# Two steps moved inside the period of an attention and FFN kernel: the denominators' reciprocals behind the first norm, the queries' transposes behind the last down tile

## The reference

```python
def layer(h, p):
    q = _phi((h @ wq + bq_).reshape(b, s, H, DH))       # _phi(t) = elu(t) + 1, 16 heads of 8
    k = _phi((h @ wk + bk_).reshape(b, s, H, DH))
    v = (h @ wv + bv_).reshape(b, s, H, DH)
    kv = jnp.einsum('bshd,bshm->bhdm', k, v)
    z = 1.0 / (jnp.einsum('bshd,bhd->bsh', q, k.sum(axis=1)) + 1e-06)
    att = jnp.einsum('bshd,bhdm,bsh->bshm', q, kv, z).reshape(b, s, d)
    h = h + att @ wo + bo_
    h = _ln(h, g1_, be1_)                               # the first norm
    y = jax.nn.gelu(h @ w1 + c1_, approximate=False) @ w2 + c2_
    return (_ln(h + y, g2_, be2_), None)                # the second norm
...
    xn = _layernorm(x, axis=-1)
    s = ...  # eight layers on xn, and a last _ln
    g = _silu(...)  # routed experts on xn
    return x + s * g
```

## Time and profile before

| what | us |
|---|---|
| median of 3 runs | 873.08 |
| lowest and highest run | 872.48 and 874.48 |
| the profiled execution | 874.67 |
| its span in the trace | 873.0 |
| TensorE, VectorE, ScalarE busy | 818.8, 795.7, 720.0 |
| mean granted clock of TensorE | 0.972 of full speed |

### The profile page before, as it was taken

One profiled execution on the slowest core, in us unless ns is written; L12 is line 12 of the kernel. 1 busy time (PEld: TensorE's weight loads), 2 busy tenths in 40 slices (PEclk: granted clock), 3 DMA queues, 4 the chain that ended last, 5 costly groups with the idle time before them and its releaser, 6 DMA issues.

```text
span 873.0 us, 19269 instructions
## 1 busy us (share of the span) xinstructions
PE 818.8 (94%) x5914; PEld 742.1 (85%) x5914; DVE 795.7 (91%) x2763; ACT 720.0 (82%) x1271; POOL 376.9 (43%) x362
## 2 busy tenths in 40 slices
PE   5698999999999999999999999999999999977776
PEld 4588899999999999999998999999999999876653
DVE  6888999989899999989899999989999989999998
ACT  2579999989998899989998899889998999654543
POOL 5234445445454444445445445354443544332113
PEclk9899999999999999999999999999999999999995
DMA  5300201010010101020010101010010000000002
GB/s 146 88 2 2 43 2 24 12 29 16 2 34 2 43 2 35 1 44 2 2 34 2 44 1 35 1 44 2 1 35 1 1 2 1 20 7 1 1 1 97
DMA packets 26264, 18.76 MB, mean 21 GB/s; under 512 B 4354, under 2 KB 22195, under 8 KB 26164
## 3 DMA queue, kind: packets, MB, share of 16 engines
q1 hardware_dynamic: 25300, 16.95, 7.4%
q10 hardware_dynamic: 864, 0.59, 0.2%
HBM read 15.43 MB, written 2.10 MB: 20 GB/s over the span
## 4 chain that ended last, share of the span: by engine, by line
PE 77%; DVE 14%; ACT 5%; issue 4%; DMA 0%; ACTq 0%; DVEq 0%
PE down_ps L749 20%; PE small_ps L682 6%; PE att_ps L712 6%; PE up_ps L741 5%; PE up_ps L739 5%; PE up_ps L740 5%; PE t_ps L660 4%; PE t_ps L719 3%; PE kq_ps L672 3%; PE kq_ps L673 3%; PE kq_ps L674 3%; DVE z_lo L1001 2%; ACT z_hi L900 2%; PE up_ps L703 2%; PE small_ps L690 2%
## 5 line engine op out<-in xcount | busy, mean ns | idle before, releaser
L749 PE MATMUL down_ps<-w_use,hid 128*128 128x128 f32 x2048 | 261.3, 276 | 0.7 <-ACT hid L851 0.7
L749 PEld LDWEIGHTS down_ps<-w_use,hid 128*128 128x128 f32 x2048 | 245.8, 193 | 1.9 <-ACT hid L851 1.1
L1019 POOL TENSOR_TENSOR res_ffn<-z_tm,g_ffn 128x512 f32<-128x512 f32 x64 | 82.7, 1292 | 265.4 <-DVE k_e L1103 240.9
L1008 POOL TENSOR_TENSOR res_att<-z_tm,g_att 128x512 f32<-128x512 f32 x64 | 82.5, 1288 | 174.3 <-DVE h L961 174.3
L851 ACT ACTIVATE hid<-up_ps 128x512 f32<-128x512 f32 x192 | 113.7, 592 | 30.7 <-PE up_ps L741 23.2
L973 DVE BATCH_NORM_STATS2 st<-h 128x6 f32<-128x128 f32 x512 | 109.1, 275 | 0.1
L906 ACT ACTIVATE z_tm<-h,shift,rstd 128x128 f32<-128x128 f32 x224 | 91.7, 482 | 0.0
L739 PE MATMUL up_ps<-z_hi,w_hi 128*128 128x512 f32 x192 | 86.2, 449 | 0.7 <-DVE z_lo L1001 0.7
L1022 POOL TENSOR_TENSOR res_ffn<-res_ffn,ffn_row 128x512 f32<-128x512 f32 x64 | 84.2, 1315 | 5.0
L1011 POOL TENSOR_TENSOR res_att<-res_att,att_row 128x512 f32<-128x512 f32 x64 | 82.4, 1287 | 5.0
L672 PE MATMUL kq_ps<-w_kq_hi,zq_hi 128*128 128x256 f32 x256 | 83.0, 324 | 1.5 <-DVE zq_lo L921 1.5
(11 more groups left out here) (191 smaller groups left out, 1964.8 us busy)
## 6 DMA issues: line engine op xcount, KB each, us to landing
raw_w<-in_L_attn_W SPq DMA_DIRECT2D x15, 256.0 KB, 4.6
out_y<-gate_tm SPq DMA_DIRECT2D x8, 256.0 KB, 2.2
bias_bc<-in_L_attn_c SPq DMA_DIRECT2D x7, 256.0 KB, 4.5
x_tm<-in_L_attn_x SPq DMA_DIRECT2D x3, 512.0 KB, 7.8
raw_rows<-in_L_attn_be SPq DMA_DIRECT2D x15, 64.0 KB, 4.1
raw_g<-in_L_attn_g SPq DMA_DIRECT2D x14, 64.0 KB, 3.2
x_tm<-in_L_attn_x SPq DMA_DIRECT2D x2, 256.0 KB, 3.3
raw_rows<-in_L_attn_bo SPq DMA_DIRECT2D x8, 64.0 KB, 4.1
```

The costliest lines, as they stand in the source:

```text
L749: last = nc.tensor.matmul(down_ps[:, t, :], hid[:, j, t * P:(t + 1) * P], w2_use[:, j, :], start=(j == 0), stop=(j == FC - 1))
```

## The change

Two calls are moved, and no instruction is added, removed or altered. On VectorE `dve_rden` goes from behind `dve_blocks` to behind `dve_norm1`. On TensorE `pe_qn_transpose` goes from before the fourth down tile to behind it. Their waits go with them. The queues of ScalarE, GpSimd and SyncE are as before.

```diff
@@ pe_period
                 pe_z1_transpose(pe, p - 1, p + 2 if state else UNITS)
+            if ffn:
+                pe_down(pe, p - 2, (3,))
             if att:
                 pe_qn_transpose(pe, p)
-            if ffn:
-                pe_down(pe, p - 2, (3,))
             if state:
@@ dve_period
                 dve_den(dve, p)
                 dve_blocks(dve, p)
-                dve_rden(dve, p)
             if b == 4 and is_layer(l + 1):
@@ dve_period
             if ln1:
                 dve_norm1(dve, p, p - 1)
             if att:
+                dve_rden(dve, p)
                 dve_q_n(dve, p)
                 dve_kvo(dve, p)
```

## The result

| | before | after |
|---|---|---|
| median of the runs, us | 873.78 (4 runs) | 894.50 (4 runs) |
| lowest and highest, us | 872.48, 875.23 | 893.31, 894.74 |
| profiled execution, us | 874.67 | 894.54 |
| its span, us | 873.0 | 892.8 |

The ratio of the runs is 1.0234, with a 95% interval from 1.0214 to 1.0254. The changed kernel is slower, inside the range of the prediction, 5 us above its value.

The account below looks back on a forecast made before the run. It took TensorE's hand-overs through ScalarE and VectorE as the bound, with ScalarE nearly as long. Six layers at +2.66, +0.8, +1.0 and -1.4 gave +16.4 on 874.67: 891.1 profiled, 889.5 us median; range 881 to 896.

Parts of the forecast that it names:

- The ring L719, z_hi, z_lo, L660: TensorE to ScalarE to VectorE and back: 2.01 us of hand-overs, plus 9.80 of TensorE, make the 11.81 us period.
- q_n starts at Z + 1.95: ScalarE's copy of the transposed queries starts 1.95 us after Z, the start of L719; 0.82 later than before.
- ScalarE has 0.59 of room: ScalarE's slack per plain period: 0.45 us idle before z_hi plus 0.14 at the second GELU, against q_n's 0.82 delay.
- its ring through rstd is 12.00: From q_n through rstd's Exp, m_r, norm and L719 back to q_n: no period after the change under 12.00 us.
- The sign of being wrong that I had named: On ScalarE, z_hi still idle by about 0.45 us in plain periods would mean room the forecast had not seen.
- the period with the rounding of W1: Period where ScalarE also rounds W1 ahead of its table load: some 0.53 us more, 12.53 us.
- The attention product waits 0.11 to 0.12 for q_n: On TensorE, L712 starts at Z + 2.61 against 2.50, adding 0.11 to 0.12 us wherever nothing else is late.
- The reciprocals behind the norm make z_lo late in a period that starts right with the norm: On VectorE, 0.69 us of reciprocals put z_lo at Z + 1.68 instead of 1.26, L660 at 2.43 instead of 2.01.
- A layer: plus 2.66: Eight periods of a middle layer walked to 99.22 us after against 96.56 before; bounds 2.3 to 3.1.
- Outside the middle layers: First layer: nothing up to about 94 us, then +0.8; last layer: first three periods +1.0, last five -1.4 us.
- TensorE's waits are taken away: Rival: TensorE is the bound and loses its waits at L703 and for the norm; at most -8.6 us, 864.5; 3%.
- The clock falls: Rival: TensorE waits in most periods, so 3% of the span runs at 1.2 GHz; +13 us, about 903; 4%.

Follow-up runs that it names:

- the short copy: Changed kernel (both moves) with ScalarE's copy q_n (L893) cut to a quarter of its columns: 886.90 us, ratio 1.0156.
- the short norm: Changed kernel (both moves) with two of the four tiles of ScalarE's second norm (L906) left out: 892.37 us, ratio 1.0208.

## Why the prediction held, and where its steps did not

The sign, the size and the range held: 891.1 was summed for the profiled execution, 894.54 measured. The account of the light periods did not hold, and that the sum came so near is in part luck. Step by step:

- *The ring L719, z_hi, z_lo, L660 bounds the kernel before, and TensorE's 9.80 us outside it.* Shown for the plain period: 0.22 us taken out of the 9.80 shorten it from 11.81 to 11.59. Two periods of a layer are held by the norm instead.
- *q_n starts at Z + 1.95.* Right: L703 at 1.33, q_n at 1.97 (432.14 against 430.17), idle before it for L703 59 times, 45.2 us in all.
- *ScalarE has 0.59 of room, and its ring through rstd is 12.00.* Wrong, and this was the step that carried my account of the light periods. I read the 0.68 between two GELUs as ScalarE's own time. It was TensorE's pace; ScalarE needs 0.48. From q_n to the Exp of rstd it takes 7.83 in the plain period that begins at 418.05 (420.01 to 427.84), and not 8.22. With 7.83 that ring is 11.61 us, less than the 11.81 of the period before the change, and ScalarE's room is 0.45 + 0.53 = 0.98 instead of 0.59, more than the 0.82 by which q_n is later. The sign of being wrong that I had named is there: z_hi still sits idle 0.47 in the plain period (430.81). m_r waits for rstd 30 times in 64, 12.3 us in all, and not every time, and the period with the rounding of W1, for which I had 12.53, takes 12.12. Relieving ScalarE of 0.77 us gave 0.38 a layer.
- *The attention product waits 0.11 to 0.12 for q_n.* The mechanism was right and its size was off. It was listed as a small bound, and it is the cost of the light periods: 0.12 at L712, 0.09 more before the next product, since L712 itself runs slower behind a wait (1.16 against 1.06), and 0.07 at the fourth up chunk, which waits for the first GELU, late by the same copy. That is 0.28, where 0.26 to 0.31 was measured, and all of it leaves when the copy is shortened. The first of the three was in the forecast, but there ScalarE's ring took it over; the last was named as an addition at the upper end.
- *The reciprocals behind the norm make z_lo late in a period that starts right with the norm.* Right up to L660: z_lo is 1.81 behind L719 (forecast 1.68) and L660 2.55 (2.43). But such periods are two of eight and not an alternation, since rstd does not bind in the others. And the path behind it was wrong. I let TensorE need 9.80 from L660 to the next L719, and in the period that begins at 442.29 it needs 10.22: L690 waits for VectorE's copy g_sb, which the reciprocals push as well, and this wait ends last. L690 is at 7.85 to 7.91 with both moves, with the reciprocals alone, and with the short copy, whether L660 is at 2.55 or at 2.80. So each such period costs 0.81 rather than 0.42.
- *A layer: plus 2.66.* Measured 3.32. By the runs it is 6 x 0.28 + 2 x 0.81 = 3.30. The light periods were forecast 0.19 longer by a ring that doesn't bind and are 0.3 longer another way. The two late ones were sized at half. Against these the 12.53 was 0.41 too high.
- *Outside the middle layers.* From the L719 at 131.10 to the one at 712.82 the change adds 19.5 us. Ahead of it the changed kernel is 1.5 us earlier, where I had forecast 0.8 us later; 1.3 of that is there in the first start of L719 already (37.19 against 38.47), which differs from run to run by as much. Behind it, +1.9 remain, where I had forecast about the same as a loss and a gain (+1.0 and -1.4). One period of the last layer is 1.39 longer than before (18.66 against 17.27), and with the short norm the one ahead of it is 18.67 where the changed kernel has 17.40; the cause of both stays open.

Of the rivals, *TensorE's waits are taken away* fell: L703's wait for q_nt did shrink from 7.2 us to 3.0, and paid nothing. That is also the answer to the rule of the Trainium skill, "Perfetto Trace Analysis", section "Identifying the Most-Contended Engine", to find the engine with the highest occupancy and optimize it first: ScalarE at 82% was no bound by its amount of work, in which the rule was right, and yet one of its copies, 0.6 us long, came onto the path by its place. Occupancy did not show it before or after. *The clock falls* fell too: the mean granted clock of the changed kernel is 0.984 of full speed against 0.972, and in the middle layers (107 to 700 us before, 107 to 715 after) it is 1.00 in both.

## What to carry to other kernels

Write down, for each wait of the bounding engine, what it hands over and what stands in the handed-over engine's queue; then see a reordering as a change of rings, not of busy times. An instruction whose result comes back through another engine should be issued early and have other work behind it; putting the filler in front of it, as here, takes the cover away from the return trip. Read the spacing of an engine's instructions where they have nothing to wait for, before you call it that engine's own cost. And when a wait has grown, look further down the same engine's queue for one that ends later: shortening the first then wins nothing.

## What the runs showed of the hardware

A 128x512 activation of ScalarE whose input is ready started 0.48 to 0.50 us behind the one before (the GELUs from 436.08 to 437.03, w_hi at 438.20 behind 437.71); the 0.68 to 0.70 between other GELUs is the pace of TensorE's up products. The copy q_n took 0.28 us on 128 columns and 0.60 on 512. A group of eight 128x128 float32 products (L712) that had waited for its input took 1.16 us against 1.06, and the next product started 0.91 behind it against 0.81, beyond the wait itself; this held for all 36 such groups between 107 and 700 us in the changed kernel. With waits of 0.1 to 0.5 us on TensorE in its periods of 12 to 13 us the granted clock stayed at 1.00 from 107 to 715 us. VectorE's w_lo took 1.47 us behind the late z_lo and 1.14 before the change; why is open.
